# Turning a third half row of E by DMA in the last row block of a two-layer graph kernel

## What is computed

```
deg  = clip(adj.sum(1), 1);  dis = deg ** -0.5
diffusion = (dis[:,None] * adj * dis[None,:]) @ x - x
sim  = x @ x.T / (norm_i * norm_j)
attn = softmax(beta * sim * adj, axis=1)
x1   = layernorm(x + diffusion + sigmoid(alpha) * (attn @ x - x))
out  = layernorm(x1 + relu(adj @ (x1 @ weights)))
```

## Time and profile before

| | |
|---|---|
| median of 3 runs | 655.35 us |
| the profiled execution | 654.72 us |
| its span from the first to the last instruction | 652.9 us |
| TensorE's granted clock over the span | 0.999 |
| PE busy | 638.8 us, 98% of the span |
| DVE, ACT, POOL busy | 516.7, 412.6, 237.4 us |

### The profile page before, as it was taken

One profiled execution on the slowest core, in us unless ns is written; L12 is line 12 of the kernel. 1 busy time (PEld: TensorE's weight loads), 2 busy tenths in 40 slices (PEclk: granted clock), 3 DMA queues, 4 the chain that ended last, 5 costly groups with the idle time before them and its releaser, 6 DMA issues.

```text
span 652.9 us, 16141 instructions
## 1 busy us (share of the span) xinstructions
PE 638.8 (98%) x5103; PEld 465.8 (71%) x5103; DVE 516.7 (79%) x1565; ACT 412.6 (63%) x768; POOL 237.4 (36%) x249
## 2 busy tenths in 40 slices
PE   8889999999999999999999999999999999999996
PEld 7456777777777777777777777888888864444465
DVE  5989999999999999999999998887777863334453
ACT  7999999999999999999999998611111110000000
POOL 5999644544544544644644647300000000000000
PEclk9999999999999999999999999999999999999999
DMA  7879999999999999999999995300000000000001
GB/s 278 310 162 256 298 236 246 289 252 244 292 251 234 297 247 251 306 241 248 299 239 251 289 252 95 73 7 0 0 0 0 0 1 1 17 16 18 16 32 33
DMA packets 165020, 107.37 MB, mean 164 GB/s; under 512 B 144384, under 2 KB 148608, under 8 KB 164992
## 3 DMA queue, kind: packets, MB, share of 16 engines
q1 hardware_dynamic: 164992, 107.04, 62.7%
HBM read 69.27 MB, written 2.10 MB: 109 GB/s over the span
## 4 chain that ended last, share of the span: by engine, by line
PE 90%; DVE 3%; ACT 2%; DMA 2%; issue 1%; POOL 1%; SPq 0%; DVEq 0%; ACTq 0%; POOLq 0%
PE ps_s L1007 23%; PE ps_s L1204 17%; PE ps_e L1176 15%; PE ps_acc L1040 8%; PE ps_e L1018 8%; PE ps_e L1040 8%; PE ps_acc L1043 4%; PE ps_e L1043 4%; DMA x_keep<-in_x 1%; DMA eTx<-e_parts 1%; DVE scores L708 1%; PE ps_e L1056 1%; ACT scores L523 1%; DVE y_parts L819 1%; PE ps_s L1056 1%
## 5 line engine op out<-in xcount | busy, mean ns | idle before, releaser
L1007 PE MATMUL ps_s<-xn_parts,xn_signed 128*128 128x512 f16 x756 | 203.3, 379 | 2.9 <-DVE cmax L708 2.9
L708 DVE CUSTOM_DVE_ANT_1 scores<-ps_s,adj_bytes 128x512 f32<-128x512 f32 x252 | 171.8, 684 | 22.3 <-PE ps_s L1007 15.3
L523 ACT ACTIVATE scores<-scores,col 128x1024 f32<-128x1024 f32 x128 | 157.3, 1232 | 1.1 <-DVE col L719 0.9
L482 ACT ACTIVATE adj_bytes<-land 128x1024 uint8<-128x1024 f32 x128 | 133.5, 1047 | 0.6 <-POOL packed L343 0.6
L351 POOL TENSOR_SCALAR e_parts<-scores 128x1024 f16<-128x1024 f32 x64 | 68.5, 1071 | 152.9 <-ACT scores L523 149.4
L1176 PE MATMUL ps_e<-y_parts,stage 128*128 128x256 f16 x896 | 98.0, 273 | 0.0
L1007 PEld LDWEIGHTS ps_s<-xn_parts,xn_signed 128*128 128x128 f16 x756 | 68.5, 98 | 38.5 <-DVE cmax L708 2.5
L1176 PEld LDWEIGHTS ps_e<-y_parts,stage 128*128 128x128 fp8e4 x896 | 87.7, 98 | 10.1
L530 ACT ACTIVATE eT_parts<-ps_e 128x512 f16<-128x512 f32 x128 | 75.9, 596 | 26.2 <-PE ps_e L1018 25.0
L723 DVE SCALAR_TENSOR_TENSOR eT_parts<-ps_e,eT_parts 128x512 f16<-128x512 f32 x128 | 87.3, 684 | 1.9 <-ACT eT_parts L530 1.9
L729 DVE SCALAR_TENSOR_TENSOR e_parts<-scores,e_parts 128x1024 f16<-128x1024 f32 x64 | 86.3, 1350 | 0.4 <-POOL e_parts L351 0.4
(11 more groups left out here) (128 smaller groups left out, 972.2 us busy)
## 6 DMA issues: line engine op xcount, KB each, us to landing
land<-in_adj SPq DMA_DIRECT2D x128, 512.0 KB, 5.4
x_keep<-in_x SPq DMA_DIRECT2D x4, 512.0 KB, 5.6
out<-u SPq DMA_DIRECT2D x7, 256.0 KB, 2.1
eTx<-e_parts SPq DMA_TRANSPOSE x64, 4.3
packT<-packed SPq DMA_TRANSPOSE x16, 7.0
out<-u SPq DMA_DIRECT2D x2, 128.0 KB, 1.7
scores<-in_L_gnn_weights SPq DMA_DIRECT2D x1, 64.0 KB, 1.9
col<-in_L_gnn_beta SPq DMA_DIRECT2D x1, 0.5 KB, 7.2
```

Source lines behind the costliest of these rows:

```text
L482: nc.scalar.activation(adj_bytes[:, q, i * CH:(i + 1) * CH], land[:, q, i, :], ACT.Copy, scale=float(BYTE_TOP[q] >> i), accum_out=deg[:, i ...
L523: nc.scalar.activation(piece, piece, ACT.Exp, bias=neg_max[q], scale=abs_beta, accum_out=csum[:, q, i:i + 1]).then_inc(exp_done, 1)
L708: nc.vector.tensor_tensor_reduce(scores[:, q, o:o + BANK].rearrange("p (k q) -> p k q", k=K), score_bank(h, r == 0 if start else False).re ...
L1007: ins = nc.tensor.matmul(score_bank(h, start), xn_signed[:, q, part, :], xn_parts[:, other, o:o + BANK], start=(part == 0 and other == 0), ...
```

## The change

Row block 31 alone is changed. Banks 2 and 3 (the chunk that has its exponential last) aren't turned by PE any more: POOL writes their high part and DVE their low part into the first half of `land` (`third`), SP issues a DMA that turns them into another part of that half (`thirdT`), and `attend` reads them there.

```diff
+    LAST_ATTEND = (0, 1, 4, 5, 6, 7, 2, 3)
+        spare = land[:, 0, :, :].rearrange("p i j -> p (i j)").bitcast(F16)
+        third = spare[:, 0:2 * CH].rearrange("p (a j) -> p a j", a=2)
+        thirdT = spare[:, 2 * CH:4 * CH].rearrange("p (t i) -> p t i", i=P)
 sync:
-            for r in range(R - G + 1, R):
-                turn_ex(r, r % 2, 1)
-                if r < R - 1:
-                    turn_ex(r + 1, (r + 1) % 2, 0)
+            turn_ex(R - 3, 1, 1)
+            turn_ex(R - 2, 0, 0)
+            turn_ex(R - 2, 0, 1)
             turn_adj(R // 2 - 1, 1)
-            sp.wait_ge(e_turned, R * TB)
+            turn_ex(R - 1, 1, 0)
+            turn_ex(R - 1, 1, 1)
+            sp.wait_ge(third_lo, 1)
+            sp.dma_start_transpose(thirdT, third.rearrange("p a j -> p (a j)")).wait_op(
+                x_loaded[0], 16, "sem-ge").then_inc(third_turned, 16)
+            sp.wait_ge(e_turned, R * TB - 2)
 gpsimd:
             ex_high(R - 1, 1, 1, place=1)
+            pool.wait_ge(exp_done, R * C)
+            pool.wait_ge(cast_done, R * C)
+            nc.gpsimd.tensor_scalar(third[:, 0, :], scores[:, 1, CH:2 * CH], E_SCALE, 1.0,
+                                    ALU.mult, ALU.mult).wait_op(sign_done, 1, "sem-ge").then_inc(third_hi, 1)
             y_rows(3)
 scalar:
             exps(R - 1, 1, 1, LAST_EXP)
-            e_high(R - 1, 2, order=LATE_ATTEND)
-            e_high(R - 1, 3, order=LATE_ATTEND)
             y_high(2)
 vector:
             ex_low(R - 1, 1, 1)
-            e_low(R - 1, 2)
-            e_low(R - 1, 3)
             y_low(2)
+            dve.wait_ge(third_hi, 1)
+            nc.vector.scalar_tensor_tensor(third[:, 1, :], scores[:, 1, CH:2 * CH], E_SCALE, third[:, 0, :],
+                                           ALU.mult, ALU.subtract).then_inc(third_lo, 1)
             attn_add(R - 2, 0)
             y_low(3)
 tensor:
             def last_attend(k):
-                attend(R - 1, 1, k, order=range(H))
+                attend(R - 1, 1, k, order=LAST_ATTEND, last=True)
             first_sums(0)
             last_attend(0)
             last_attend(1)
-            turn_e(R - 1, 1, 2, order=LAST_EXP)
-            turn_e(R - 1, 1, 3, order=LAST_EXP)
             first_sums(1)
-            last_attend(2)
-            last_attend(3)
             first_sums(2)
-            for k in range(4, H):
+            for k in range(2, 6):
                 last_attend(k)
-            first_sums(3)
+            sums(0, 3)
+            last_attend(6)
+            last_attend(7)
+            sums(1, 3)
+            sums(2, 3)
```

More of the change, by code:

```diff
@@ L177, in two_layer_gnn @@
         ex_turned = [sem(f"ex_turned{n}") for n in range(2)]
+        third_hi = sem("third_hi")
+        third_lo = sem("third_lo")
+        third_turned = sem("third_turned")
         attn_part = sem("attn_part")
@@ L1020, in turn_e, with attend @@
                 ins.then_inc(e_turned, 1)
-            def attend(r, q, k, start=False, early=False, order=ATTEND_ORDER):
+            def attend(r, q, k, start=False, early=False, order=ATTEND_ORDER, last=False):
                 b = order[k]
-                if b < TB:
+                if last and b in (2, 3):
+                    pe.wait_ge(third_turned, 16)
+                elif b < TB:
                     pe.wait_ge(e_lo, r * TB + (b + 1))
@@ L1035, in attend @@
                     t, slot = TH * b + SLOT[n], TH * (b % 2) + n
-                    if b < TB:
+                    if last and b in (2, 3):
+                        hi, lo = (thirdT[:, a * TC + slot, :] for a in range(2))
+                    elif b < TB:
                         hi, lo = (eT_parts[:, b, a, n * P:(n + 1) * P] for a in range(2))
```

## The result

The changed kernel takes 657.64 us, the median of eight runs (655.8 to 659.22), beside 655.40 for the kernel before in the same comparison: a ratio of 1.0032 [1.0021, 1.0042], so slower by 0.2 to 0.4%, some 2.1 us. A ninth execution, of 1168.05 us at a granted clock of 0.652, is not counted. The time lies inside the range on record (654.7 to 657.7), 0.06 us from its upper end, and 1.24 us above the forecast of 656.4; the outcome held likeliest, "within 0.2%", did not come.

A forecast was written before the change was run, and what follows sets the result against it. PE's own work was taken to bound the kernel (90% of the chain). Terms -0.88 - 0.53 + 2.44 = +1.03 us gave 655.75 against the profiled 654.72, and 656.4 on the runs' median of 655.35; range 654.7 to 657.7.

The forecast's parts named there:

- within 0.2%: Outcome that the measurement can't tell the changed kernel from no change, 0.2% being 1.31 us; chance 0.65.
- The chain of collisions: DVE's low parts and POOL's operations after 414 take turns on one port, so `y_low(2)` ends at 420.05.
- S: Start of PE's `first_sums(2)`, once `y_low(2)` is ready: 420.10 instead of 417.66, a new wait of 2.44 us.
- The sum: Shift of PE's `sums(3, 0)`: -0.88 - 0.53 + 2.44 = +1.03 us, starting at 429.30 instead of 428.27.
- -0.88 of the transposes: Eight transposes removed from PE, all on the path: 0.88 us saved.
- -0.53 of the old waits: PE's two waits, for `e_low` at 418.65 and for `y_low(2)`, gone if nothing came late: 0.53 us saved.
- What comes late next: DMA turns after the new wait: no PE wait for the first two; third lands 425.6, upper end costing 0.5 us.
- DVE keeps the port: Rival: DVE passes waiting POOL, `first_sums(2)` starts at 417.66, but PE waits for DMA turns: +0.6, 656.0; chance 0.18.
- as meant: Rival: DVE passes POOL, third low part goes ahead of `y_rows(3)`, PE waits 0.55 and 0.3: 654.8; chance 0.15.
- third rival: PE's clock falls to 1.2 GHz behind the new wait at `first_sums(2)`: +1 to +2 on top, 657.4 to 658.4; chance 0.15.
- slower: Outcome that the changed kernel measures slower than the kernel before by more than about 0.2%; chance 0.29.

The follow-up runs named there:

- hi_act_gate: The changed kernel with the third high part written by ACT instead of POOL, and `y_rows(3)` held until the third low part is written: 655.49 us, 0.9996.
- a_again: The changed kernel once more, no edit, for more executions and a second profile: 658.08 us, 1.0035.
- pin_after: The changed kernel with POOL's third `y_rows` held until `y_low(0)` is written: 657.40 us, 1.0029.
- y_gate: The changed kernel with POOL's `y_rows(3)` held until the third low part is written: 656.30 us, 1.0006.
- pin_fill: The changed kernel with POOL's third `y_rows` held until `y_low(0)` is written, and nine unused dummy products between `first_sums(1)` and `first_sums(2)`: 656.16 us, 1.0013.

## Why the prediction was right and where it failed

**The chain of collisions: right, each step to 0.05 us.** Forecast and profile: `y_low(1)` ends 414.15 and 414.14; the high part 416.19 and 416.18; `ex_low(1)` 417.26 and 417.25; `y_rows(3)` 418.98 and 419.01; `y_low(2)` 420.05 and 420.08; S 420.10 and 420.14. The step that no row of before showed, that a waiting POOL gets in between two DVE operations that stand back to back, is shown by `ex_low` at 3.19 us and, the other way round, by the 2.35 us once POOL's high part is gone. Both runs agree with the Trainium skill's rule of an exclusive lock (SBUF — State Buffer, "SBUF: two separate sides"); whose turn comes next, which decided the sum here, is read from these rows.

**The sum: right on the profiled execution.** +1.03 forecast, +1.09 in the profile. The -0.88 of the transposes and the -0.53 of the old waits are really gone: with the wait away, `hi_act_gate` gains 0.46 in spite of some 0.9 us for the second and third turns, read from one start to the next.

**What comes late next: right.** The third turn was issued at 421.29 (forecast 421.3) and took 4.3 us to land, so 425.6 as forecast, and PE never waited for a DMA. The cases "DVE keeps the port" and "as meant" fell with the 3.19 us.

**The step that failed is the weight of the third rival.** The mechanism, the place and the price of "the clock falls" are what the runs show: 1.67 us in the profile of `a_again`, where +1 to +2 stood. But it was given 0.15, as a question of yes or no ("it decides if the wait at S, whose length lies between those two idle stretches, brings the clock down"). It is a question of how often: one and the same wait of 2.3 us brings the clock down in some executions and not in others. The mean clock was 0.997 or less in six of the eight executions of the first comparison, in six of the twelve of `a_again`, and in seven of the twelve of `pin_after`. In the kernel before it was so in three of the 93 executions that the experiments' ratios are taken from (0.997 twice, and 0.995 in one of 658.43 us), in `y_gate` and `hi_act_gate` in none of 24. So it is about half, or more, and that decides the median. The forecast's 656.4 was the time of a kernel that waits and keeps its clock: it is near what `pin_fill` measured, 656.16. With a half on this rival, "slower" would have been the likeliest outcome by the prediction's own prices.

**The range: in part luck.** It holds the measured median by 0.06 us, and its upper end was set by shares in which the clock had 0.15. The second comparison's 658.08 us, beside 655.92 for the kernel before there, lies outside it.

**What stays open.** Only profiled executions show where the clock was low; that the others with a low mean lost it at the same place is inferred from their times. On which condition it falls was not settled. Nor do clock and wait explain every execution: 659.22 in the first comparison kept a clock of 1.0, and on the chip of `a_again` executions at 0.998 took up to 660.01, while the kernel before reached 658.43 there. The toss at `y_low(0)`, worth 1.4 to 1.6 us of waiting where it was lost, is one candidate, shown in two profiles but not counted over executions. Another lies ahead of the change: PE's last wait for a turn of row block 30 ends between 405.05 and 406.47 us in the thirteen profiles, so up to 1.4 us of the difference between two executions is there before the changed stretch begins.

## What to carry to other kernels

Work moved off the bounding engine is a gain only as far as the engines it goes to have room in that order: here 1.41 us of saved work and waits went into two meetings of POOL and DVE on one port, which could be worked out to 0.05 us from rows far from the place. A new wait in a stretch where PE was busy throughout has a second price, the clock behind it, and it comes in a part of the executions only, so one profile can miss it: look at the granted clock of every execution before trusting the profiled one. What took the loss away was to keep POOL out of DVE's way there: holding `y_rows(3)` back was enough to bring the time to the kernel before's (1.0006 [0.9993, 1.0019]), putting it first was not (1.0022). A gain beyond that, with the work given to ACT and to a gap of DVE, is small: 0.9988 [0.9979, 0.9997].

## What the runs showed of the hardware that was not expected

- After the same wait of PE (2.32 and 2.33 us) in the same program, the granted clock over the four microseconds from 420 was 1.00 in one execution and 0.60 in another. With 18 instructions of no use in the wait it was 1.00 in the profiled execution, and the mean clock was 0.998 or more in all eleven.
- A waiting engine gets the port between two operations of the other that follow on each other without a gap, in either direction, and the one that lost waits through the whole of the other's operation: 1.21 became 2.91 us for `y_low(2)`, 1.08 became 1.94 for POOL's high part.
- A product of two fp32 operands of 128x128 counts as two instructions of PE, of 0.12 us each (18 in 2.17); a transpose by the same identity counts as one (eight in 1.04).
